# An ODE layer beside an eigenvector recurrence: its matrix scaled first, longer turns, and merge-tree signs without levels

## The chip, the core and the metric

The kernel runs on one core of one Trainium2 chip. The metric is device time in microseconds from launch to end; lower is better. The program is eight layers over one activation tensor, and the change touches one stage of it.

## What is computed

The input `x` has shape (16, 512, 128), the adjacency `adj` (512, 512). Each layer adds its result to `x`. Two layers meet in the stage of this case: layer L1's graph part, eight Euler steps of an ODE, and the eigenvectors `U` that layer L2's graph part needs, which depend on `adj` alone and are computed beside the earlier layers.

```python
def _L1_gnn_ref(x, adj_mx, alpha_train, w, d, fc_in_w, fc_in_b, vt):
    ...
    h = jnp.einsum('bnd,ed->bne', x, fc_in_w) + fc_in_b
    alph = jax.nn.sigmoid(alpha_train)[:, None]
    ...
    def euler_step(h, _):
        ax = jnp.einsum('nm,bmd->bnd', adj_mx, h)
        f = alph * 0.5 * (ax - h) + h @ w_eff - h + x0
        return (h + dt * f, None)
...
    _, U = jnp.linalg.eigh(L_norm)
...
    x = x + _L1_gnn_ref(_layernorm(x, axis=-1), adj, L1_gnn_alpha_train, L1_gnn_w, L1_gnn_d, L1_gnn_fc_in_w, L1_gnn_fc_in_b, 0)
```

## The kernel before, in words

`eigenvectors` (L757) has two stages before its last one. The first finds the eigenvalues of a tridiagonal matrix by counting sign changes. The second, the `nc.Block` at L1140, is the stage of this case. It turns eigenvalues into eigenvectors `Z` (512 per partition, four column blocks `NB` = 4), nearly all on VectorE (DVE):

- **entry** (L1161 to L1187): a root and some scaling, among it L1181, which scales the 128x2048 matrix `V` that only the next stage reads;
- **recurrence** (L1207 to L1225): 512 steps `n`, each of three dependent 128x8 operations (L1213, L1221, L1223), and every 16 steps two operations for the next diagonals `dn` (L1202);
- **selection and scans** (L1233 to L1289): wide operations; then the squared norms go to ScalarE (ACT) at L1295, which takes their root at L1155, and DVE goes on at L1297 with `dve.wait_ge(root_out, 2)`;
- **merge tree** (L1317 to L1441): signs are decided level by level for blocks of 16, 32, ... 256 entries. Each of the five levels issues 48 DVE operations on 128x64, 128x32, ... 128x4 elements, and every one waits for the one ahead of it. At the end L1443 gives `Z` its signs.

Beside it runs class `Ode` (L2783). TensorE (PE) does its matrix work, ACT copies results out of PSUM, and DVE does small pieces of it in between its own steps:

- `Ode.start` (L2835), on DVE, ahead of the recurrence: 64 `bn_stats` (L2840) for the layer norm of `X`; then `wTd` (L2845), the scaled matrix `L1` (L2852, L2855), mean and deviation (the root on ACT, L2992), and `rstd` (L2883).
- **prelude** on PE: four transposes of `L1` (L3027) as soon as all four blocks are there, then 512x512 products for its second, third and sixth power (L3033), small products for powers `R` of the weights (L3039) and rows for the bias (L3062, L3067, L3072). They wait for DVE through `r_in`, `fr_in` and `row_in`.
- **turns**: 17 of them (L3076 to the end of `tensor`), number -1 for the constant term `KC`, then 0 to 15 for the batches. In a turn PE waits for `YT` from ACT, does 12 matmuls of 384 columns (L3083), four transposes (L3089) once DVE's four row blocks (L2889, semaphore `x_full`) are there, then L3095 and L3102 twice. In turn -1 the weights of L3083 are one row of one partition. ACT copies between them (L3007, L3004, L3010, L3015).
- DVE's pieces come from the generator `vector` (L2892). `side.tick()` stands after each recurrence step and after most operations behind it. `yield n` in the generator means that the next piece follows n ticks later, and a turn takes `TURN` = 29 ticks. In a turn DVE does four row blocks, adds `KC` to `X` (L2959) and adds the result of the turn before (L2967). What is left is issued by `side.finish()` at the end.

ACT's program in this stage is `side.scalar(act)`, all of the ODE's copies, between the roots of L1152 and L1155. Its instructions run in that order:

```python
                    nc.scalar.activation(t1[:, :], t1[:, :], ACT.Sqrt).then_inc(root_out, 1)
                    side.scalar(act)
                    act.wait_ge(root_in, 2)
                    nc.scalar.activation(LO[:, :], LO[:, :], ACT.Sqrt).then_inc(root_out, 1)
```

The stage ends for all engines together, when DVE is through and all 16 results are added (`dve.wait_ge(side.added, B)`).

## Time and profile before

| what | value |
|---|---|
| median of 3 runs | 6687.58 us (6683.04 to 6689.84) |
| the profiled execution, its own time | 6687.53 us |
| its span, first to last instruction | 6685.5 us |
| busy: TensorE, VectorE, ScalarE, GpSimd | 79%, 68%, 35%, 1% |
| mean granted TensorE clock | 0.936 |
| the stage of this case | 4078.4 us to 4664.8 us of the span |

All times in what follows are microseconds from the start of the span, unless they are lengths. In a row of a timeline the first number is the start, the second how long the row took (of "x64", all 64 together), and square brackets hold the idle time ahead of it on its engine and what ended it. The profile gives a matmul of f32 as two records, so L3083's 12 matmuls read x24.

### The profile page before, as it was taken

To read this page: it belongs to the slowest core of one execution; us is meant where nothing else is said; L and a number is where in the kernel's file an instruction comes from. 1 tells how busy PE (TensorE), PEld (TensorE's weight loads), DVE (VectorE), ACT (ScalarE), POOL (GpSimd) and SP (SyncE) were. 2 spreads that over 40 slices of the span, in tenths; PEclk is the share of its full clock that TensorE was granted. 3 is DMA by queue.
4 is the path that set the end of the run, shared out by engine and by line. 5 is a ranking of instruction groups with operands and counts; after the bars stand their busy time and mean duration, and the time that the engine had idled before them with its cause. 6 is when DMAs were issued, how large, how long until landed. Compare 5 with 4: busy or idle time off the path is not lost. (4 is left out here: it accounts for less than half of the span.)

```text
span 6685.5 us, 109379 instructions
## 1 busy us (share of the span) xinstructions
PE 5302.8 (79%) x33047; PEld 3780.1 (57%) x33047; DVE 4555.0 (68%) x26992; ACT 2314.4 (35%) x7376; POOL 93.3 (1%) x128
## 2 busy tenths in 40 slices
PE   4666788888877769969899995995573689976999
PEld 4555566666666535446566662663351367745676
DVE  7888888888888863359999998778445333345333
ACT  2222222222222224529598893110020133311333
POOL 0000000000000000000000000000000000000000
PEclk9999999999999999969999997997786889986999
DMA  1000000000000000010000000000010000000000
GB/s 47 2 2 2 2 3 5 3 4 4 3 4 4 4 21 13 7 54 4 5 6 5 6 3 8 1 1 1 1 51 1 13 0 0 0 10 14 0 0 25
DMA packets 27827, 56.64 MB, mean 8 GB/s; under 512 B 6185, under 2 KB 16834, under 8 KB 25538
## 3 DMA queue, kind: packets, MB, share of 16 engines
q1 hardware_dynamic: 27330, 50.79, 2.2%
q8 instruction: 216, 3.54, 0.2%
q14 instruction: 281, 2.30, 0.1%
HBM read 38.20 MB, written 12.58 MB: 8 GB/s over the span
## 5 line engine op out<-in xcount | busy, mean ns | idle before, releaser
L2007 DVE SCALAR_TENSOR_TENSOR f_ACC<-f_yp,f_CG,f_ACC 128x128 f32<-128x128 f32 x1024 | 288.4, 344 | 461.6 <-DVEq L2005 461.6
L1952 PEld LDWEIGHTS f_yp<-f_W,f_hs 128*128 128x128 f32 x4096 | 490.1, 192 | 92.5 <-issue 91.8
L1886 PE MATMUL f_hp<-f_rows,f_W 128*128 128x512 f32 x1024 | 532.3, 602 | 4.8 <-ACT U L1896 2.7
L1983 ACT ACTIVATE f_hs<-f_hp,f_b 128x512 f32<-128x512 f32 x512 | 347.6, 685 | 539.9 <-ACTq L1982 539.9
L710 PE MATMUL h_small<-h_part,ones 128*128 128x2 f32 x1024 | 300.8, 363 | 294.1 <-DVE h_jd L579 198.1
L1054 ACT ACTIVATE e_XD<-e_X,e_scal 128x60 f32<-128x60 f32 x2048 | 527.7, 333 | 17.5 <-DVEq L918 15.7
L655 ACT ACTIVATE h_VW<-h_v,h_s 128x8 f32<-128x8 f32 (+3 forms) x512 | 154.9, 302 | 1082.4 <-DVE h_s L417 1082.4
L1942 PE MATMUL f_hp<-f_XT,f_W 128*128 x1024 | 484.5, 601 | 33.1 <-PEq L2236 33.1
L703 PEld LDWEIGHTS h_ax<-h_XM,h_parts 128*128 128x128 bf16 x11520 | 481.0, 114 | 40.9 <-issue 40.9
L1952 PE MATMUL f_yp<-f_W,f_hs 128*128 128x128 f32 x4096 | 493.5, 275 | 0.0
L710 PEld LDWEIGHTS h_small<-h_part,ones 128*128 128x128 f32 x1024 | 256.8, 312 | 414.7 <-DVE h_jd L579 287.2
L703 PE MATMUL h_ax<-h_XM,h_parts 128*128 128x3 bf16 x11520 | 407.9, 167 | 30.0 <-DVE h_parts L170 30.0
L678 PE MATMUL h_small<-h_part,ones 128*128 128x2 f32 x1024 | 300.5, 363 | 159.4 <-DVE h_jb L337 122.0
L678 PEld LDWEIGHTS h_small<-h_part,ones 128*128 128x128 f32 x1024 | 256.7, 311 | 289.2 <-DVE h_jb L337 232.7
L692 PE MATMUL h_sr<-h_sums,ones 128*128 128x1 f32 (+15 forms) x1024 | 314.9, 397 | 79.6 <-DVE h_parts L170 42.5
L1876 PEld LDWEIGHTS f_yp<-f_W,UT 128*128 128x128 f32 x2048 | 267.4, 195 | 187.6 <-issue 92.6
L1876 PEld LDWEIGHTS f_yp<-f_W,U 128*128 128x128 f32 x2048 | 268.6, 192 | 113.9 <-issue 92.8
L692 PEld LDWEIGHTS h_sr<-h_sums,ones 128*128 128x128 f32 x1024 | 256.9, 311 | 104.3 <-issue 48.6
L1876 PE MATMUL f_yp<-f_W,UT 128*128 128x128 f32 x2048 | 281.5, 282 | 40.5 <-ACT UT L1896 32.2
L2754 PE MATMUL g_PG<-g_HL,g_Wih 128*128 128x256 f32 (+2 forms) x624 | 291.8, 625 | 21.9 <-DMA g_bhh<-in_g_bhh 18.0
L641 ACT ACTIVATE h_s<-h_small 128x1 f32<-128x1 f32 x512 | 87.7, 171 | 580.4 <-PE h_small L678 579.7
L939 DVE SCALAR_TENSOR_TENSOR e_PB<-e_PB,e_scal,e_u 128x60 f32<-128x60 f32 x1024 | 283.1, 276 | 0.0
(715 smaller groups left out, 11303.0 us busy)
## 6 DMA issues: line engine op xcount, KB each, us to landing
f_S<-in_f_W SPq DMA_DIRECT2D x64, 128.0 KB, 2.3
X<-in_x SPq DMA_DIRECT2D x1, 4096.0 KB, 16.4
held<-g0e_HL SPq DMA_DIRECT2D x16, 256.0 KB, 2.0
g_HL<-held SPq DMA_DIRECT2D x16, 256.0 KB, 2.8
f_W<-in_f_W SPq DMA_DIRECT2D x2, 2048.0 KB
spill<-f_xts SPq DMA_DIRECT2D x16, 256.0 KB, 2.0
f_rows<-spill SPq DMA_DIRECT2D x16, 256.0 KB, 2.6
f_W<-in_f_W SPq DMA_DIRECT2D x4, 1024.0 KB
```

Source lines behind the costliest of these rows:

```text
L678: nc.tensor.matmul(tot[j % 2], C.ones[:, :], part[:, 0:2], start=True, stop=True).then_inc(tot_out, 1)
L692: nc.tensor.matmul(sr[:, 0:n], C.ones[:, :], sums[:, 0:n], start=True, stop=True).then_inc(sr_out, 1)
L703: ins = nc.tensor.matmul(ax[:, m, 0:3], A_part[:, b, m * P:(m + 1) * P], XB[:, q, b, 2 * XC + 1:2 * R2 + 2:2], start=(b == ph and n == 0), ...
L710: nc.tensor.matmul(dots, C.ones[:, :], part[:, 2:4], start=True, stop=True).then_inc(dots_out, 1)
L1054: ins = nc.scalar.activation(XD[b][:, k, h, :], X[:, :], ACT.Identity, bias=scal[b][:, k, 2 * h:2 * h + 1])
L1876: ins = nc.tensor.matmul(self.yp[d % 3][:, 0:D], self.hs[unit % 2][:, j, i * P:(i + 1) * P], self.W2[:, unit % E * FC + j, :], start=(j == ...
L1886: nc.tensor.matmul(self.hp[s % 3][:, :], self.W1[:, e, j * P:(j + 1) * P], self.rows[:, g % 2, :], start=True, stop=True).then_inc(self.h_ ...
L1942: nc.tensor.matmul(hp[:, u % 2, c, :], W1[:, col // F, col % F:col % F + P], rows_t, start=True, stop=True).then_inc(h_full, 1)
L1952: ins = nc.tensor.matmul(yp[:, u % 2, k, :], hs[:, u % 2, c, k * P:(k + 1) * P], W2[:, u * UC + c, :], start=(c == 0), stop=(c == UC - 1))
L1983: nc.scalar.activation(hs[:, u % 2, c, :], hp[:, u % 2, c, :], func, bias=b1[:, u * UC + c:u * UC + c + 1]).then_inc(hs_full, 1)
L2007: ins = V_.scalar_tensor_tensor(ACC[:, k, :], yp[:, u % 2, k, :], CG[:, k * E + e:k * E + e + 1], ACC[:, k, :], ALU.mult, ALU.add)
L2754: ins = nc.tensor.matmul(o2, Wih[:, p - 1, gi * D:(gi + 1) * D], x, start=True, stop=(t == 0))
```

## The change

Three parts, in one stage.

**The order at its start.** `side.start` stands ahead of L1181 and no longer holds the 64 `bn_stats`. These and the rest of the layer norm are in a new `side.statistics`, behind the scaling of `V`. Row 1 and row 2 of the weight powers are made there, not in ticks. ACT takes the deviation's root behind the copies of `L1T` and `L2T`.

```diff
@@ -1178,6 +1188,7 @@
                     dve.wait_ge(ch, done.next())
                     V_.tensor_tensor(G[:, :], rad[:, :], t1[:, :], ALU.mult).then_inc(ch, 1)
                     dve.wait_ge(ch, done.next())
+                    side.start(dve)
                     V_.tensor_tensor(V[:, :, :], V[:, :, :], G[:, :].unsqueeze(1).broadcast_to([P, NB, N]), ALU.mult).then_inc(ch, 1)
                     dve.wait_ge(ch, done.next())
                     V_.memset(EB[:, 0:1], 0.0).then_inc(ch, 1)
@@ -1186,8 +1197,32 @@
                     done.next()
                     V_.memset(one[:, :], 1.0).then_inc(ch, 1)
                     dve.wait_ge(ch, done.next())
-                    side.start(dve)
+                    side.statistics(dve)
                     side.begin(dve)
```

**The pacing of the ODE's pieces.** `TURN` goes from 29 to 34, with 12 more in turn -1. The generator waits fewer ticks ahead of the powers (12 and 6 in place of 4, 17, 17 and 17). The one copy of `Fr` moves behind the products of `Gm`. Single ticks behind wide operations become 2, 4 or 6.

```diff
@@ -2784,7 +2816,7 @@


     STEPS = 8
-    TURN = 29
...
@@ -2835,10 +2867,6 @@
     def start(self, dve):

         V_, ch, done, C = self.nc.vector, self.ch, self.done, self.C
-        st, a, b, v, mean, rstd = (t[:, :] for t in (self.st[:, :, 0], self.a, self.b, self.v, self.mean, self.rstd))
-        for t in range(T):
-            V_.bn_stats(self.st[:, t, :], self.X[:, t, :]).then_inc(ch, 1)
-            done.next()
...
             V_.scalar_tensor_tensor(blk, C.ident[:, :], self.a78[:, n:n + 1], blk, ALU.mult, ALU.add).then_inc(self.l1_made, 1)
+        V_.tensor_copy(self.R[:, 0, :], C.ident[:, :]).then_inc(ch, 1)
+        done.next()
+
+    def statistics(self, dve):
+
+        V_, ch, done = self.nc.vector, self.ch, self.done
+        a, b, v, mean, rstd = (t[:, :] for t in (self.a, self.b, self.v, self.mean, self.rstd))
+        dve.wait_ge(self.r_out, 1)
+        V_.tensor_scalar(self.R[:, 1, :], self.PR[:, 0:D], 1.0 / self.STEPS, None, ALU.mult).then_inc(self.r_in, 1)
+        for t in range(T):
+            V_.bn_stats(self.st[:, t, :], self.X[:, t, :]).then_inc(ch, 1)
+            done.next()
+        dve.wait_ge(ch, done.n)
...
         V_.tensor_tensor(v, a, b, ALU.add).then_inc(self.var_in, 1)
-        V_.tensor_copy(self.R[:, 0, :], C.ident[:, :]).then_inc(ch, 1)
-        done.next()
+        self.wider_power(dve, 0)
...
+    def wider_power(self, dve, k):
+
+        lo, hi = ((2, 3), (3, 5), (5, 9))[k]
+        dve.wait_ge(self.r_out, k + 2)
+        self.nc.vector.tensor_copy(self.R[:, lo:hi, :].rearrange("p m d -> p (m d)"), self.PR[:, 0:(hi - lo) * D]).then_inc(self.r_in, 1)
...
@@ -2893,18 +2939,14 @@

         V_, ch, done, C, STEPS = self.nc.vector, self.ch, self.done, self.C, self.STEPS
         R, Gm, Fr, PR, TY = self.R, self.Gm, self.Fr, self.PR, self.TY
-        dve.wait_ge(self.r_out, 1)
-        V_.tensor_scalar(R[:, 1, :], PR[:, 0:D], 1.0 / STEPS, None, ALU.mult).then_inc(self.r_in, 1)
         for n in range(NB):
             ins = self.row_block(0, n)
             if n == NB - 1:
                 ins.then_inc(self.x_full, 1)
             yield 2
-        yield 4
-        for k, (lo, hi) in enumerate(((2, 3), (3, 5), (5, 9))):
-            dve.wait_ge(self.r_out, k + 2)
-            V_.tensor_copy(R[:, lo:hi, :].rearrange("p m d -> p (m d)"), PR[:, 0:(hi - lo) * D]).then_inc(self.r_in, 1)
-            yield 17
+        for k in (1, 2):
+            self.wider_power(dve, k)
+            yield 12 if k == 1 else 6
...
                     ins.then_inc(self.fr_in, 1)
             yield 2
-        dve.wait_ge(self.frow_out, 3)
-        V_.tensor_copy(Fr[:, STEPS, :], PR[0:1, 0:D]).then_inc(ch, 1)
-        done.next()
...
                 if k % 4 == 3:
                     yield 1
+        yield 3
+        dve.wait_ge(self.frow_out, 3)
+        V_.tensor_copy(Fr[:, STEPS, :], PR[0:1, 0:D]).then_inc(ch, 1)
+        done.next()
+        yield 9
...
                 V_.tensor_tensor(xs, xs, self.HS[(turn - 1) % 2], ALU.add).then_inc(self.added, 1)
-            yield self.TURN - used
+            yield self.TURN + (self.LEAD if turn < 0 else 0) - used
...
-    def tick(self):
-
...
+    def tick(self, times=1):
+
+        for _ in range(times):
+            if self.pause > 0:
+                self.pause -= 1
+            if self.pause == 0:
+                self.pause = next(self.work, -1)
...
         nc.scalar.activation(self.al[:, :], self.al[:, :], ACT.Sigmoid).then_inc(self.sg, 1)
-        act.wait_ge(self.var_in, 1)
-        nc.scalar.activation(self.sd[:, :], self.v[:, :], ACT.Sqrt).then_inc(self.sd_out, 1)
         for out, made, full in ((self.L1T, self.l1t_out, self.l1t_in), (self.L2T, self.l2t_out, self.l2t_in),
                                 (self.L3T, self.l3t_out, self.l3t_in), (self.L3, self.l3_out, self.l3_in),
                                 (self.L6T, self.l6t_out, self.l6t_in)):
+            if out is self.L3T:
+                act.wait_ge(self.var_in, 1)
+                nc.scalar.activation(self.sd[:, :], self.v[:, :], ACT.Sqrt).then_inc(self.sd_out, 1)
```

```diff
                         done.next()
-                        side.tick()
+                        side.tick(2)
                     dve.wait_ge(ch, done.n)
                     V_.tensor_tensor(g1[:, :, :], bwd, g1[:, :, :], ALU.subtract).then_inc(ch, 1)
-                    side.tick()
+                    side.tick(6)
                     dve.wait_ge(ch, done.next())
                     V_.scalar_tensor_tensor(g1[:, :, :], g1[:, :, :], -1.0, g1[:, :, :], ALU.mult, ALU.max).then_inc(ch, 1)
...
                         V_.memset(t2[:, 0:1], 0.0).then_inc(ch, 1)
-                        side.tick()
                         dve.wait_ge(ch, done.next())
                         V_.scalar_tensor_tensor(t2[:, 1:N], ES[:, 0:N - 1], -1.0, R[:, N - 2::-1, NB + jb], ALU.mult, ALU.mult).then_inc(ch, 1)
-                        side.tick()
+                        side.tick(2)
                         dve.wait_ge(ch, done.next())
                         V_.tensor_tensor_scan(Z[:, jb, :], t2[:, :], t1[:, :], 0.0, ALU.mult, ALU.add).then_inc(ch, 1)
-                        side.tick()
+                        side.tick(2)
```

**The merge tree.** What depends on `ES` and the tolerances alone is made ahead of the recurrence. All 31 nodes of the five levels stand side by side in tensors of 31 per column block (128x124). Everything but the signs is computed for all of them at once, with waits only where an input needs one. A node's sign is written as `sa * (sb * p + r) + (sb * s + q)`, and only these six operations are done level by level.

```diff
                     V_.tensor_tensor(g1[:, :, :], Z[:, :, :], Z[:, :, :], ALU.mult).then_inc(ch, 1)
-                    dve.wait_ge(ch, done.next())
-                    V_.tensor_reduce(mass[:, :, :], g1[:, :, :].rearrange("p j (s w) -> p j s w", w=LEAF), AX.X, ALU.add).then_inc(ch, 1)
-                    dve.wait_ge(ch, done.next())
+                    done.next()
                     V_.memset(sg[:, :, :], 1.0).then_inc(ch, 1)
-                    dve.wait_ge(ch, done.next())
...
-                        size *= 2
...
+                    side.tick(2)
+                    dve.wait_ge(ch, done.n)
+                    V_.tensor_tensor(host[:, :, :], ma, mb, ALU.is_ge).then_inc(ch, 1)
+                    host_made = done.next()
+                    V_.tensor_tensor(a2[:, :, :], va[:, :, :], vb[:, :, :], ALU.subtract).then_inc(ch, 1)
+                    a2_made = done.next()
+                    V_.tensor_tensor(mx[:, :, :], ma, mb, ALU.mult).then_inc(ch, 1)
+                    mx_made = done.next()
+                    V_.tensor_tensor(mh[:, :, :], ma, mb, ALU.max).then_inc(ch, 1)
+                    mh_made = done.next()
+                    V_.tensor_scalar(st[:, :, :], tt[:, :, :], 0.0, -2.0, ALU.is_ge, ALU.mult).then_inc(ch, 1)
+                    st_made = done.next()
+                    dve.wait_ge(ch, max(host_made, a2_made))
+                    V_.tensor_tensor(a2[:, :, :], a2[:, :, :], host[:, :, :], ALU.mult).then_inc(ch, 1)
+                    a2_made = done.next()
+                    dve.wait_ge(ch, mx_made)
+                    V_.tensor_scalar(mx[:, :, :], mx[:, :, :], tol[:, 0:1], 0.64, ALU.mult, ALU.mult).then_inc(ch, 1)
+                    mx_made = done.next()
+                    dve.wait_ge(ch, mh_made)
+                    V_.tensor_scalar(mh[:, :, :], mh[:, :, :], tol[:, 0:1], None, ALU.mult).then_inc(ch, 1)
...
+                    dve.wait_ge(ch, max(mx_made, k2_made))
+                    V_.scalar_tensor_tensor(sp[:, :, :], k2[:, :, :], -1.0, mx[:, :, :], ALU.mult, ALU.mult).then_inc(ch, 1)
+                    done.next()
+                    V_.scalar_tensor_tensor(sq[:, :, :], k2[:, :, :], 1.0, mx[:, :, :], ALU.subtract, ALU.mult).then_inc(ch, 1)
+                    done.next()
+                    side.tick(4)
+                    for size, lo, hi in levels:
+                        w = hi - lo
+                        dve.wait_ge(ch, done.n)
+                        V_.tensor_tensor(x1[:, :, 0:w], sb_[:, :, lo:hi], sp[:, :, lo:hi], ALU.mult).then_inc(ch, 1)
+                        u_made = done.next()
+                        V_.tensor_tensor(mh[:, :, 0:w], sb_[:, :, lo:hi], ss[:, :, lo:hi], ALU.mult).then_inc(ch, 1)
+                        w_made = done.next()
+                        dve.wait_ge(ch, u_made)
+                        V_.tensor_tensor(x1[:, :, 0:w], x1[:, :, 0:w], sr[:, :, lo:hi], ALU.add).then_inc(ch, 1)
+                        u_made = done.next()
+                        dve.wait_ge(ch, w_made)
+                        V_.tensor_tensor(mh[:, :, 0:w], mh[:, :, 0:w], sq[:, :, lo:hi], ALU.add).then_inc(ch, 1)
+                        w_made = done.next()
+                        dve.wait_ge(ch, u_made)
+                        V_.tensor_tensor(x1[:, :, 0:w], x1[:, :, 0:w], sa[:, :, lo:hi], ALU.mult).then_inc(ch, 1)
+                        u_made = done.next()
+                        dve.wait_ge(ch, max(u_made, w_made))
+                        V_.tensor_tensor(sg[:, :, LEAVES + lo:LEAVES + hi], x1[:, :, 0:w], mh[:, :, 0:w], ALU.add).then_inc(ch, 1)
+                        done.next()
+                        side.tick(2)
+                    dve.wait_ge(ch, done.n)
                     for jb in range(NB):
-                        V_.tensor_scalar(Z[:, jb, :], Z[:, jb, :], sg[:, jb, 0:1], None, ALU.mult).then_inc(ch, 1)
-                        dve.wait_ge(ch, done.next())
+                        V_.tensor_scalar(Z[:, jb, :], Z[:, jb, :], sg[:, jb, 2 * LEAVES - 2:2 * LEAVES - 1], None, ALU.mult).then_inc(ch, 1)
+                        done.next()
```

How this moves the instructions, at three places. **DVE at the stage's entry**, where `e_Z` is the matrix `L1` and `t_V` is `V`. Before:

```order
L1181 TENSOR_TENSOR t_V<-t_V,t_G 128x2048 [waits e_chain]
L1183 MEMSET e_EE 128x1 [waits e_chain]
L1185 COPY e_EE<-e_EE 128x511
L1187 MEMSET e_one 128x8
L2840 BN_STATS g_st<-X 128x6 [waits e_chain]
L2840 BN_STATS g_st<-X 128x6 x63
L2843 TENSOR_SCALAR g_d<-g_d 128x1 [waits g1_loaded]
L2845 TENSOR_SCALAR g_wTd<-g_wT,g_d 128x128 [waits g1_ch]
L2847 TENSOR_SCALAR g_a<-g_al 128x4 [waits g1_sg]
L2849 TENSOR_SCALAR g_a<-g_a 128x4 [waits g1_ch]
L2852 TENSOR_SCALAR e_Z<-e_Z,g_a 128x512 [waits g1_ch]
L2855 SCALAR_TENSOR_TENSOR e_Z<-ident,g_a,e_Z 128x128 [waits g1_ch]
```

and now, from the fourth and last block of the matrix on (L2880, L2883):

```order
L2880 TENSOR_SCALAR e_Z<-e_Z,g_a 128x512
L2883 SCALAR_TENSOR_TENSOR e_Z<-ident,g_a,e_Z 128x128 [waits g1_ch]
L2884 COPY e_g<-ident 128x128
L1192 TENSOR_TENSOR t_V<-t_V,t_G 128x2048
L1194 MEMSET e_EE 128x1 [waits e_chain]
L1196 COPY e_EE<-e_EE 128x511
L1198 MEMSET e_one 128x8
L2892 TENSOR_SCALAR e_g<-g_PR 128x128 [waits g1_r_out,e_chain]
L2894 BN_STATS g_st<-X 128x6 x64
L2898 TENSOR_TENSOR g_ln_a<-g_st 128x64 [waits g1_ch]
```

The scaled matrix now stands ahead of the scaling of `V` and of the statistics.

**ACT**, whose `g_ln_sd` is the deviation of the layer norm and `e_LO` the root of the squared norms. The change, at the start of the stage:

```order
L3035 ACTIVATE g_al<-g_al 128x4 [waits g1_loaded]
L3044 COPY g_L1T<-g_Q 128x512 [waits g1_l1t_out] x4
L3044 COPY U<-g_Q 128x512 [waits g1_l2t_out] x4
L3041 ACT_TABLE_LOAD
L3041 ACTIVATE g_ln_sd<-g_ln_v 128x64 [waits g1_var_in]
L3044 COPY g_L3T<-g_Q 128x512 [waits g1_l3t_out] x4
```

and at its end:

```order
L3050 COPY g_YT<-g_TY 128x512 [waits g1_ty_out]
L3053 COPY UT<-g_Q 128x512 [waits g1_q_out]
L3056 COPY UT<-g_Q 128x512 [waits g1_v_out]
L3061 COPY UT<-g_Q 128x512 [waits g1_added,g1_h_out]
L1165 ACTIVATE e_LO<-e_LO 128x4 [waits e_root_in]
```

The root of the deviation moved behind eight copies. The root of `e_LO` is where it was, last, behind every copy of the ODE.

**DVE, the last level of the signs and the end** (`s_sg` are signs). Now:

```order
L1456 TENSOR_TENSOR s_w<-s_sg,s_w 128x4 [waits e_chain]
L1458 TENSOR_TENSOR s_w<-s_sg,s_w 128x4
L1461 TENSOR_TENSOR s_w<-s_w 128x4 [waits e_chain]
L1464 TENSOR_TENSOR s_w<-s_w 128x4 [waits e_chain]
L1467 TENSOR_TENSOR s_w<-s_w,s_sg 128x4 [waits e_chain]
L1470 TENSOR_TENSOR s_sg<-s_w 128x4 [waits e_chain]
L1475 TENSOR_SCALAR e_Z<-e_Z,s_sg 128x512 [waits e_chain]
L1475 TENSOR_SCALAR e_Z<-e_Z,s_sg 128x512 x3
L3011 TENSOR_TENSOR X<-X,UT 128x512 [waits g1_hs_in,g1_ch]
```

A level issues 6 operations here, where it issued 48, and the last addition to `X` is now behind the signs.

## Rows read from the trace of the kernel before

**Rows 1.** The page's first line.

```profile
span 6685.5 us, 109379 instructions
```

**Rows 2.** Stretches: length, busy time (instructions) of PE, PEld, DVE, ACT, POOL, PE clock, DMA.

```profile
4078.40:4665.00 586.60, 450.99 (x1978) 285.34 (x1978) 452.89 (x2182) 72.82 (x126) 0.00 (x0) 0.88 0.01 3
4603.77:4662.53 58.76, 0.00 (x0) 0.00 (x0) 50.16 (x249) 0.00 (x0) 0.00 (x0) 0.50 0.00 0
```

**Rows 3.** Waits of DVE in the stage: us in total, times, longest.

```profile
DVE g_XG L2889 <- PE g_TY L3102: 58.2, 14, 12.7
```

**Rows 4.** Timeline of DVE in the entry: scaling of `V`, then the ODE's first operation.

```profile
4087.04 2.29 DVE L1181 TENSOR_TENSOR t_V<-t_V,t_G 128x2048 f32<-128x2048 f32 x1
...
4102.24 0.13 DVE L2843 TENSOR_SCALAR g_d<-g_d 128x1 f32<-128x1 f32 x1
```

**Rows 5.** Groups of the entry on DVE: busy, mean ns of one, idle before.

```profile
L2840 DVE BATCH_NORM_STATS2 g_st<-X 128x6 f32<-128x128 f32 x64 | 12.5, 273 | 0.0
```

**Rows 6.** Timeline of PE in the prelude, from its second bias row to turn -1.

```profile
4157.14 1.86 PE L3062 MATMUL g_PR<-e_g,g_fbC 128*1 128x512 f32 x2 [12.06 <-DVE e_g L2924]
4158.93 15.01 PE L3033 MATMUL g_Q<-g_L3T,UT 128*128 128x512 f32 x32
...
4177.52 3.60 PE L3072 MATMUL g_TY<-g_L6T,ones 128*1 128x512 f32 x8
4186.11 15.72 PE L3083 MATMUL g_Q<-e_g,U 1*128 1x384 f32 x24 [4.99 <-DVEq L2944]
```

**Rows 7.** Timeline of ACT in the prelude.

```profile
4084.64 1.28 ACT L2992 ACT_TABLE_LOAD   x1
...
4125.12 0.58 ACT L2998 COPY U<-g_Q 128x512 f32<-128x512 f32 x1 [2.85 <-PE g_Q L3033]
```

**Rows 8.** Timeline of DVE in the prelude: weights `Gm`, then the first bias row.

```profile
4152.60 0.64 DVE L2913 TENSOR_SCALAR g_Gm<-g_TY 128x128 f32<-128x128 f32 x3
...
4156.28 0.80 DVE L2924 TENSOR_SCALAR e_g<-g_PR 1x128 f32<-1x128 f32 x4
```

**Rows 9.** Timeline of DVE in a turn: row blocks, an addition, two plain steps.

```profile
4243.47 0.29 DVE L2889 TENSOR_SCALAR g_XG<-X,g_mean,g_rstd 128x128 f32<-128x128 f32 x1
...
4244.20 0.30 DVE L2889 TENSOR_SCALAR g_XG<-X,g_mean,g_rstd 128x128 f32<-128x128 f32 x1
4244.41 0.16 DVE L1213 SCALAR_TENSOR_TENSOR e_t<-e_QR,e_EE 128x8 f32<-128x8 f32 x1
...
4245.48 0.16 DVE L1213 SCALAR_TENSOR_TENSOR e_t<-e_QR,e_EE 128x8 f32<-128x8 f32 x1
...
4246.12 0.17 DVE L1213 SCALAR_TENSOR_TENSOR e_t<-e_QR,e_EE 128x8 f32<-128x8 f32 x1
```

**Rows 10.** Timeline of PE: the first matmuls of turns 0 and 1.

```profile
4218.82 8.01 PE L3083 MATMUL g_Q<-g_Gm,g_YT 128*128 128x384 f32 x24 [0.68 <-ACT g_YT L3004]
...
4242.45 8.01 PE L3083 MATMUL g_Q<-g_Gm,g_YT 128*128 128x384 f32 x24 [0.68 <-ACT g_YT L3004]
```

**Rows 11.** Stretches of turn -1 and turn 0 on PE: length, busy, PE clock, DMA.

```profile
4186.10:4201.80 15.70, 15.69 (x25) 0.50 0.00 1
...
4218.80:4226.80 8.00, 7.98 (x26) 1.00 0.00 0
```

**Rows 12.** Timeline: ACT's last copy of the ODE, DVE at the root.

```profile
4590.44 0.58 ACT L3015 COPY UT<-g_Q 128x512 f32<-128x512 f32 x1 [3.93 <-PE g_Q L3095]
...
4599.76 0.17 DVE L1295 COPY e_LO<-e_q 128x4 f32<-128x4 f32 x1
...
4600.20 0.18 DVE L1297 RECIPROCAL e_q<-e_LO 128x4 f32<-128x4 f32 x1 [0.27 <-ACT e_LO L1155]
```

**Rows 13.** Timeline of DVE in the merge tree, first level, and its end.

```profile
4612.26 0.23 DVE L1361 TENSOR_TENSOR s_w<-s_w 128x64 f32<-128x64 f32 x1
4612.52 0.23 DVE L1363 TENSOR_TENSOR s_w<-s_w 128x64 f32<-128x64 f32 x1
...
4662.53 2.05 DVE L1443 TENSOR_SCALAR e_Z<-e_Z,s_sg 128x512 f32<-128x512 f32 x4
```

More of the change, by code:

```diff
@@ new lines, in _ @@
+                    V_.tensor_reduce(mass[:, :, 0:LEAVES], g1[:, :, :].rearrange("p j (s w) -> p j s w", w=LEAF), AX.X, ALU.add).then_inc(ch, 1)
+                    mass_made = done.next()
+                    V_.tensor_tensor(tt[:, :, :], vb[:, :, :], st[:, :, :], ALU.mult).then_inc(ch, 1)
+                    made = done.next()
+                    V_.tensor_tensor(vb[:, :, :], vb[:, :, :], vb[:, :, :], ALU.mult).then_inc(ch, 1)
+                    vb_made = done.next()
+                    dve.wait_ge(ch, made)
@@ new lines, in _ @@
+                    side.tick(2)
+                    dve.wait_ge(ch, done.n)
[6 more added lines that the diff above has]
+                    V_.tensor_tensor(mh[:, :, :], ma, mb, ALU.max).then_inc(ch, 1)
@@ new lines, in _ @@
+                    x1_made = done.next()
+                    dve.wait_ge(ch, a2_made)
+                    V_.scalar_tensor_tensor(a2[:, :, :], a2[:, :, :], 2.0, bb4, ALU.mult, ALU.mult).then_inc(ch, 1)
+                    a2_made = done.next()
+                    dve.wait_ge(ch, st_made)
+                    V_.tensor_scalar(st[:, :, :], st[:, :, :], 1.0, None, ALU.add).then_inc(ch, 1)
+                    st_made = done.next()
+                    side.tick(4)
+                    dve.wait_ge(ch, max(a2_made, mh_made))
@@ new lines, in _ @@
+                    side.tick(4)
+                    for size, lo, hi in levels:
+                        w = hi - lo
[15 more added lines that the diff above has]
+                        V_.tensor_tensor(sg[:, :, LEAVES + lo:LEAVES + hi], x1[:, :, 0:w], mh[:, :, 0:w], ALU.add).then_inc(ch, 1)
+                        done.next()
+                        side.tick(2)
@@ L2938, in vector @@
                     yield 1
+        yield 3
+        dve.wait_ge(self.frow_out, 3)
+        V_.tensor_copy(Fr[:, STEPS, :], PR[0:1, 0:D]).then_inc(ch, 1)
+        done.next()
+        yield 9
         for j in (1, 2):
```

219 lines of the change are left out of this document (93 added, 126 removed).

## The prediction, made before the change was run

> **What bounds the kernel now.** I first asked which part of the span the change can touch. It is one stage of 586.6 us out of 6685.5, with DVE busy 452.9 and PE 451.0 of it [rows 1, 2]. Nothing of any other stage moves, and a barrier closes this one, so the question is only when the stage ends. The waits of DVE come next. It sat idle for 58.2 us in 14 waits of its row blocks for PE [rows 3]: in each turn of the ODE DVE is done first and waits. PE's turns follow each other every 23.63 us [rows 10], and PE waits 0.68 at each start, for ACT. So in the recurrence PE is the bound and DVE waits. Then it turns round. ACT's last copy of the ODE ends at 4591.0, and DVE comes to the root only at 4599.8 [rows 12]. From there on PE is idle and DVE alone runs until 4664.6: 64.4 us, of which the merge tree takes 58.8 for 249 instructions [rows 2, 12, 13]. The stage's end is therefore: PE's turns, then a gap of 9 us, then DVE's tail.
>
> **The chain after the change.** DVE arrives at the root earlier, since the longer turns let it do five more steps per turn in place of waiting. A turn of DVE is now 34 steps of 0.64 us, 21.8; four row blocks add 0.09 each (0.73 against 0.64), two additions 0.43 each (1.07 against 0.64) [rows 9], and the diagonals about 0.3. Together 23.3, just under PE's 23.63. By the same count the old 29 steps are 20.1, and 13 waits of 3.5 and one of 12.7 are the 58.2 of the row. Without them DVE would arrive at 4599.8 - 58.2 = 4541.6, give or take a few microseconds for pieces that move. But the root on ACT still stands behind all of the ODE's copies, so DVE cannot pass it before the last turn is over. What was hidden becomes a wait of some 24 us. The new chain is: scaled matrix, PE's prelude, 17 turns, ACT's last copy and root, DVE's tail. So I need three sizes: how much earlier turn -1 starts, what it costs, and how long the tail is. Adding up DVE's savings (58 in the turns, 42 in the tail) would count 24 us that the root gives back.
>
> **1. The scaled matrix comes first: 15.2 us.** Its first operation goes from 4102.24 to 4087.04, where the scaling of `V` began [rows 4]. This takes 64 `bn_stats` (12.5 [rows 5]), the scaling (2.3) and two short ones from in front of PE. They aren't gone, they lie beside PE's first products. The deviation's root is now late: it waits for ACT's eight copies, the last of which ended at 4125.7 before, so 4110.5 now, and for a table load of 1.28 [rows 7]. With the root, the five operations behind it and 13 small ones for the tree's constants (an estimate of 3.4) the recurrence starts at about 4115.2. DVE pays for that out of its 24.
>
> **2. The rest of the prelude: 3.1 and 4.2 us.** PE's second bias row waits for DVE's first four `Fr` operations. They now stand behind 30 steps, `Gm` behind 27. 27 steps are 17.3, and the pieces between them about 1.8, so `Gm` starts at 4134.3; from there to the end of `Fr` it was 4152.60 to 4157.08, 4.5 [rows 8]. So PE goes on at 4138.8 in place of 4157.14 [rows 6], 18.3 earlier, 3.1 more than the start gave: most of the wait of 12.06 stays. From there PE's own work to its last bias row took 24.0 (4157.14 to 4181.12), then it waited 4.99 [rows 6]. The products of `Gm` that held it up are done earlier now; a copy of one row and the hand-over stay, some 0.8. Turn -1 starts at 4138.8 + 24.0 + 0.8 = 4163.6 in place of 4186.1: **22.5 us earlier**. The first 2 us of the product in this stretch ran at half clock (15.01 for 32 records); a wait of another length can move this by 2 either way.
>
> **3. Turn -1: 3 us, between 0 and 7.7.** Its matmuls with weights of one row took 15.72 for 24 records at half the clock, 1.2 GHz; the same count at 2.4 GHz takes 8.01 [rows 6, 11]. PE had idled 4.99 ahead of them. Now it idles 0.8, behind work at the full clock, so it should enter at 2.4 GHz. But for 15.7 us of unbroken work the clock did not rise [rows 11], so such matmuls don't seem to hold it either, and it will fall on the way. I take 3, nearer to the row of the same matmuls than to the full gain. The Trainium skill, TensorE: Matmul & The Clock Gate (What's actually happening), says that the clock is set by how busy PE has been of late, and that a busy PE gets 2.4 GHz. By it this turn would run at the full clock and the sum would be 6606; this trace disagrees, with 15.69 of 15.70 us busy at 0.50.
>
> The sixteen turns behind it don't change, since DVE's 23.3 stays under 23.63, and its row blocks are wanted only 7.8 into PE's turn. The end of the ODE goes from 4591.0 to 4591.0 - 22.5 - 3 = 4565.5, and with the root (0.3 to DVE's next operation) DVE goes on at 4565.8 in place of 4600.2.
>
> **4. The tail: 64.4 becomes 22.8, 41.6 us.** A chained operation of 128x64 takes 0.23 and the next starts 0.26 after it [rows 13]. An operation that waits for nothing starts before the one ahead of it ends: 64 `bn_stats` of 273 ns are busy for 12.5 us in all, one each 195 ns [rows 5], and four row blocks add little to their steps. In the new order I count 91 operations. Up to the scaled `Z` nothing changes but one addition: 3.6. The squares 2.2, a memset and ten copies at 0.1 each 1.2, an addition 0.6, the reduction 2.2: 6.2. Then 28 operations on 124 elements, an estimate of 0.29 each from the row of 64 elements and one ns for each element more, but each 0.08 under the next, so 5.9, and four sums of masses 0.5. Five levels of signs with six short operations, 0.9 each, 4.5. Signs into `Z` 1.6, the last addition 0.65. Sum 22.9, rounded in the parts to 22.8. If nothing overlapped, some 70 of them would cost 0.12 more each: 8.3.
>
> The Trainium skill speaks against this part: VectorE: DVE Perf Modes (Rules for kernel authors, and The DRAIN you can't avoid) says that a drain between Vector operations comes whether or not they wait for a semaphore, and that their count matters, not their waits. By it the tail would be those 8.3 longer and the kernel 6619.5. The trace disagrees at `bn_stats`, and the page's own section on two instructions with no wait between them allows the earlier start.
>
> **Sum.** The stage ends at 4565.8 + 22.8 = 4588.6 in place of 4664.6: 76.0 us less. Against the profiled execution's own 6687.5 that is 6611.5; its time is that of the median (6687.58), so nothing is to be shifted. The recounted parts lie on either side of it by half a microsecond; I say 6611.
>
> **The rivals.**
> - *Turn -1 at the full clock* (7%): 4.7 us better than I take, 6606. For it: PE enters warm. Against it: [rows 11].
> - *Waits cost nothing, so dropping them gives nothing* (5%): 6619.5. Against it: [rows 5].
> - *The prelude stays as long as it was* (6%): a new wait of PE, or a product at half clock behind its idle time. The 7.3 us of part 2 and the 3 of part 3 are lost, 6622. For it: PE still waits on DVE's ticks there, about 9 us, and the root of the deviation is now on DVE's way.
> - *The root doesn't hold DVE* (2%): DVE's own pace sets the end, 4541.6 + 0.4 + 22.8 = 4565 and 6588. It would need ACT to be through with the ODE at 4541.6; the order of ACT's instructions speaks against it.
> - *Slower: DVE becomes late in every turn and the clock falls in each* (2%). 34 steps leave 0.3 us of a turn. If the row blocks came late, PE would idle in each turn; an idle time of 4.99 was followed by half clock, one of 0.68 was not [rows 6, 10]. With the clock down at each L3083 the sixteen turns cost 16 x 7.7 = 123 us, the sum turns from -76 to +47, 6734. It decides from an idle time of about 5 us per turn, so with steps of about 0.79 us and not 0.64 [rows 9].
> - That the change doesn't do what it says I hold for excluded: the new order has the matrix first and six operations in a level.
>
> **How the numbers follow.** The forecast has 77%. Its own bounds are 2 for the clock in the prelude, 1.5 for the 30 steps, 3 and 4.7 for turn -1, 1 for the tail, and the three runs before lie 7 us apart. This gives 6603 to 6620, which also holds the cases of 6606 and 6619.5; that leaves out about 1 in 7. A measurement here tells no more than about 0.2% (13 us) from no change, and only the slower case and unnamed mishaps are not better by that: faster 0.97, within 0.2% 0.01, slower 0.02.
>
> **What would show it.** In the new profile: the first transposes of PE at 4091; the second bias row near 4139; the first matmul of turn -1 near 4163.6, and the clock's stretch over it between 0.5 and 1.0; turns of 23.63 still; the waits of DVE for its row blocks under 6 us in all in place of 58.2; a new wait of DVE at the root of about 24 us for ACT; the stage from there in 22.8. Wrong would be: a wait of PE for `x_full`, no wait at the root, or operations of the tail that start only after the one ahead has ended.

## The result, and the profile after

The median is 6611.9 us of 4 runs (6609.02 to 6614.83), against 6688.7 of 4 runs of the kernel before: a ratio of 0.9886, 95% interval 0.9869 to 0.9904. The forecast was 6611 in a range of 6603 to 6620. The profiled execution took 6609.97, its span is 6607.7.

The page's first line of the changed kernel, which answers to [rows 1]:

```profile
span 6607.7 us, 109220 instructions
```

Its stage, from DVE's first operation (4079.92) to DVE's last end, and then the part from the root on, as stretches with the columns of [rows 2]:

```profile
4079.80:4590.20 510.40, 451.69 (x1978) 285.62 (x1978) 420.04 (x2021) 72.94 (x126) 0.00 (x0) 0.94 0.01 3
4567.60:4590.10 22.50, 0.00 (x0) 0.00 (x0) 21.79 (x91) 0.00 (x0) 0.00 (x0) 0.60 0.00 0
```

PE does the same 1978 matmul records and is busy 451.7 us with them, before 451.0. DVE has 161 instructions fewer in the stage. **Places in the stage are from here on counted from DVE's first operation in it** (4078.51 before, 4079.92 after), because each execution enters the stage at another moment. So counted, the stage was 586.1 and is 510.2: 75.9 less, where the working had 76.0. The span lost 77.8: the stage was entered 1.4 later, and what stands behind it took 2017.6 in place of 2020.9, with the same instructions. More on that below.

The waits of DVE in the stage (us in total, times, longest), which answer to [rows 3]:

```profile
DVE e_q L1331 <- ACT e_LO L1165: 26.7, 1, 26.7
DVE g_XG L2935 <- PE g_TY L3148: 3.9, 10, 1.9
DVE g_rstd L2915 <- ACT g_ln_sd L3041: 3.5, 1, 3.5
```

The 58.2 us of waits for PE are 3.9, and the root, where DVE waited 0.27, now holds it for 26.7. The timeline of the entry, the prelude, turn -1 and the first two turns, to be laid beside [rows 4, 6, 10]:

```profile
4088.44 0.15 DVE L2871 TENSOR_SCALAR g_d<-g_d 128x1 f32<-128x1 f32 x1
...
4092.52 3.67 PE L3073 MATMUL g_Q<-ident,e_Z 128*128 128x128 f32 x16 [2.75 <-DVE e_Z L2883]
...
4131.27 3.32 PE L3102 MATMUL g_TY<-e_g,g_fc 128*128 128x512 f32 x4 [2.72 <-DVE e_g L2930]
...
4139.51 1.86 PE L3108 MATMUL g_PR<-e_g,g_fbC 128*1 128x512 f32 x2 [3.66 <-DVE e_g L2966]
4141.31 16.03 PE L3079 MATMUL g_Q<-g_L3T,UT 128*128 128x512 f32 x32
...
4165.34 11.85 PE L3129 MATMUL g_Q<-e_g,U 1*128 1x384 f32 x24 [0.83 <-DVEq L2988]
...
4195.24 8.01 PE L3129 MATMUL g_Q<-g_Gm,g_YT 128*128 128x384 f32 x24 [0.68 <-ACT g_YT L3050]
...
4218.88 8.01 PE L3129 MATMUL g_Q<-g_Gm,g_YT 128*128 128x384 f32 x24 [0.68 <-ACT g_YT L3050]
```

The first matmuls of turn -1 took 11.85 in place of 15.72, and turn 0 takes 23.64 as before. And the end of the stage, which answers to [rows 12, 13]:

```profile
4566.88 0.58 ACT L3061 COPY UT<-g_Q 128x512 f32<-128x512 f32 x1 [3.93 <-PE g_Q L3141]
...
4567.60 0.18 DVE L1331 RECIPROCAL e_q<-e_LO 128x4 f32<-128x4 f32 x1 [26.71 <-ACT e_LO L1165]
...
4582.26 0.28 DVE L1439 TENSOR_TENSOR s_w<-s_w 128x124 f32<-128x124 f32 x1
4582.46 0.28 DVE L1442 SCALAR_TENSOR_TENSOR s_w<-s_w 128x124 f32<-128x124 f32 x1
...
4589.40 0.68 DVE L3011 TENSOR_TENSOR X<-X,UT 128x512 f32<-128x512 f32 x1
```

Two operations of 0.28 start 0.20 apart: the second begins before the first has ended. From the root on DVE does 91 operations, where the kernel before did 263 in its 64.4 us.

### The profile page after: what moved, and what is told of

It is laid out like the page before. It is cut to its first block and busy times, and to the rows that moved or that the text cites. A ratio compares the mean times of both kernels' runs of the same rounds, so it can differ in the third digit from the quotient of the medians.

```text
span 6607.7 us, 109220 instructions
## 1 busy us (share of the span) xinstructions
PE 5302.0 (80%) x33047; PEld 3776.1 (57%) x33047; DVE 4521.4 (68%) x26831; ACT 2314.0 (35%) x7376; POOL 93.3 (1%) x128
## 5 line engine op out<-in xcount | busy, mean ns | idle before, releaser
L1054 ACT ACTIVATE e_XD<-e_X,e_scal 128x60 f32<-128x60 f32 x2048 | 527.7, 333 | 17.5 <-DVEq L918 15.7
L2786 PE MATMUL g_PG<-g_HL,g_Wih 128*128 128x256 f32 (+2 forms) x624 | 294.1, 628 | 21.4 <-DMA g_bhh<-in_g_bhh 17.5
```

Source lines behind the costliest of these rows:

```text
L1054: ins = nc.scalar.activation(XD[b][:, k, h, :], X[:, :], ACT.Identity, bias=scal[b][:, k, 2 * h:2 * h + 1])
L2786: ins = nc.tensor.matmul(o2, Wih[:, p - 1, gi * D:(gi + 1) * D], x, start=True, stop=(t == 0))
```

## The experiments

The table gives for each kernel, in us from the start of the stage: the start of turn -1, the end of ACT's last copy of the ODE, DVE's first operation behind the root, and the end of the stage; then the median of the runs. A median with one run is marked 1x. Each ratio, with its 95% interval, is to executions of the kernel before that ran beside that kernel (their medians lie between 6685.8 and 6691.8), so it can differ a little from the quotient of two medians of the table.

| kernel | turn -1 | ODE's end | root | stage | median | ratio |
|---|---|---|---|---|---|---|
| before | 107.6 | 512.5 | 521.7 | 586.1 | 6688.7 | |
| changed | 85.4 | 487.5 | 487.7 | 510.2 | 6611.9 | 0.9886 (0.9869 to 0.9904) |
| tree_only | 110.6 | 515.8 | 524.9 | 546.3 | 6656.7 | 0.9953 (0.9939 to 0.9966) |
| no_tree | 83.1 | 485.2 | 485.4 | 551.1 | 6651.4 | 0.9944 (0.9931 to 0.9958) |
| stats_first | 96.0 | 498.2 | 498.4 | 520.8 | 6630.0 | 0.9912 (0.9898 to 0.9925) |
| turn29_single | 85.3 | 487.5 | 502.3 | 523.2 | 6629.1 | 0.9903 (0.9888 to 0.9918) |
| tree_chained | 85.1 | 487.2 | 487.4 | 521.5 | 6629.4 | 0.9907 (0.9892 to 0.9922) |
| root_early | 85.4 | 487.5 | 462.9 | 488.7 | 6596.1 | 0.9857 (0.9842 to 0.9873) |
| root_early_turn37 | 85.4 | 487.5 | 462.9 | 488.7 | 6594.0 | 0.9848 (0.9833 to 0.9863) |
| root_early_prelude | 81.8 | 483.9 | 460.0 | 485.0 | 6589.3 | 0.9849 (0.9835 to 0.9862) |
| bias_rows_later | 74.1 | 477.9 | 453.4 | 479.1 | 6580.4 | 0.9845 (0.9832 to 0.9859) |
| full_rows | 85.4 | 481.2 | 481.4 | 503.8 | 6613.0 (1x) | |
| uneven_turns | 85.4 | 529.0 | 504.5 | 530.2 | 6635.2 (1x) | |
| tree_only_again | 110.5 | 515.7 | 524.7 | 546.1 | 6650.3 (1x) | |

**1. The tree alone.** The kernel before, with the part of the change on the merge tree only, `TURN` as it was. Of the pacing's diff it has this alone, since the new tree calls `tick` with a number:

```diff
-    def tick(self):
+    def tick(self, times=1):
```

> The kernel before with the new merge tree alone (its constants ahead of the recurrence; the old order at the entry, turns of 29). My theory (ODE, then root, then DVE's tail, the savings in series): DVE still comes to the root at 4600 and the tail shrinks by 41.6, so about 6646. Rival, that an operation costs the same with and without a wait ahead of it: the tail is 8.3 longer, about 6655. In the trace: the tail from the root 22.5 to 23 us; the waits of DVE for its row blocks still 58 or so, less the 1.3 of the constants that they now hide.

The stage is 39.8 shorter. The tail is 21.4 in place of 64.4, 43.0 less (the last addition to `X` is ahead of it here). But the ODE ends 3.3 later than before: the 13 small operations for the tree's constants, 1.3 us, stand ahead of everything DVE owes PE in the prelude, and PE's second bias row starts 2.5 later. They are not hidden by the waits, as I had expected; DVE's waits for its row blocks come later and are still 58.3. Outside the stage this execution took 8.9 us more (8.4 of them behind it), which is why the median is nearer to what the rival gave. The stage decides: the rival wanted a tail 8.3 longer than 22.5, and it is 21.4.

**2. All but the tree.** The changed kernel, with the old tree back, and the constants that it makes itself gone from ahead of the recurrence:

```diff
-                    for size, lo, hi in levels:
-                        V_.tensor_copy(be[:, lo:hi], ES[:, :].rearrange("p (s w) -> p s w", w=2 * size)[:, :, size - 1]).then_inc(ch, 1)
-                        be_made = done.next()
...
+                    while size < N:
+                        m = N // size // 2
...
```

> The changed kernel with the old merge tree (new order at the entry, turns of 34 kept). My theory: the ODE ends as early as in the changed kernel and the root still waits for it, so only the old tail of 64.4 comes back: 6688.7 - 34 = about 6654.5; with the tree alone the two savings add up to the whole. Rival, that 58 us of removed waits of DVE are worth something by themselves: under 6640. In the trace: a wait at the root of 26.7 us as in the changed kernel.

The stage is 35.0 shorter than before, DVE waits 26.7 at the root. Alone, the two halves give 39.8 and 35.0, together 74.8 of the 75.9. The ODE's end is 27.3 earlier than before, and the gap from there to the root shrinks from 9.2 to 0.1. These 9 are all that the 58 us of waits gave: the earlier end of the ODE comes from the entry, the prelude and turn -1.

**3. The order at the entry.**

```diff
+                    side.bn(dve)
+                    side.start(dve)
                     side.statistics(dve)
```

(`bn` holds the 64 `bn_stats`; `side.start` is taken from ahead of the scaling of `V`, and on ACT the deviation's root stands first again.)

> The changed kernel with the old order at the entry: scaling of V and the 64 bn_stats ahead of the scaled matrix, the deviation's root ahead of ACT's copies. My theory: PE starts 15.2 us later and all that hangs on it, so 6612 + 15.2 = about 6627, and the wait at the root shrinks only by what DVE itself loses less. Rival, that the order at the entry is worth nothing because DVE's own work sets the end: 6612. A third, that PE's wait for the bias rows takes some of it back, since DVE's pieces are now nearer to what PE needs: 6612 + 9 or so.

PE's transposes start 15.3 later, as counted. Turn -1 starts only 10.6 later, and the stage is 10.7 longer. The third case came out: with PE later, DVE's pieces come in time. PE's wait for the third power (2.72) is gone, and the matmuls behind it run in 1.88 and not 3.32. So in the final kernel the order at the entry is worth 10.7 of the stage. The 15.2 were right for the start and too much for what it brings in this prelude. The median says more, 18.1: the profiled execution entered the stage 1.7 later and took 6.4 more behind it than the one of the changed kernel (on that part see the last section).

**4. Turns of 29.**

```diff
-    TURN, LEAD = 34, 12
+    TURN, LEAD = 29, 17
...
-                        side.tick(2)
+                        side.tick()
```

> The changed kernel with turns of 29 steps and single ticks behind the wide operations, as before; turn -1 keeps its 46 ticks. My theory: the ODE ends at the same place of the stage (487.5 behind its start), DVE waits 3.5 per turn again and comes to the root at about 496, so the stage is 8 to 9 longer and the time about 6620: of 58 us of waits only these 9 were ever worth anything while the root stands last. Rival, that the longer turns carry the change: the waits of about 55 come back in the time, 6660 or more.

The ODE ends at the same 487.5, DVE waits 44.5 us in 13 turns, and comes to the root at 502.3. The stage is 13.0 longer. So the mechanism holds (44.5 us of waits cost 13.0), and my size for it was 4 to 5 too small. I had moved DVE's arrival before (521.3) by the 25 that turn 0 starts earlier. But DVE also has fewer steps behind it when the turns begin: its 100th reciprocal starts at 122.7 before, 17.6 ahead of turn 0, and here at 117.0, 1.7 behind turn 0. That is 19.3 less of a lead; 13.7 of it come back in the turns (waits of 44.5 in place of 58.2), and the other 5.6 make 496.4 into the 502.0 at which DVE came to the root.

**5. A wait ahead of each operation of the new tree.**

```diff
+                    dve.wait_ge(ch, done.n)
                     V_.tensor_tensor(mx[:, :, :], ma, mb, ALU.mult).then_inc(ch, 1)
```

> The changed kernel with a wait ahead of every operation of the new merge tree, as the old one had; the operations are the same. My theory: what starts 0.08 ahead of the other's end now starts 0.03 behind it, so the tail from the root grows from 22.5 by about 8.3 to 30.8, and the time by as much, to about 6620. Rival, that only the number of operations counts: the tail stays at 22.5 and the time at 6612.

The tail from the root is 34.1 in place of 22.5: 11.7 more. DVE in this tail, wide operations of the same kind as above:

```profile
4572.83 0.29 DVE L1375 TENSOR_TENSOR s_w<-s_w 128x124 f32<-128x124 f32 x1
4573.22 0.29 DVE L1379 TENSOR_TENSOR s_w<-s_w 128x124 f32<-128x124 f32 x1
4573.55 0.29 DVE L1382 TENSOR_TENSOR s_w<-s_w 128x124 f32<-128x124 f32 x1
```

They start 0.32 to 0.33 or 0.39 apart, not 0.20. 0.33 is about what I had counted (the end of the one, and 0.03); 0.39 is where the added wait stands beside one that was already there. The page counts 51 instructions more (109271 against 109220), all of them waits, and 51 at 0.07 are 3.6 of the 11.7; the other 8.1 are close to the 8.3 of the expectation. The number of operations on DVE is the same (91), so the rival is refuted: waits between operations of 128x4 to 128x124 cost. The stage is 11.3 longer than in the changed kernel; the median is 17.5 above, so some 6 of it lie outside the stage.

**6. The root earlier.** On ACT, in `Ode.scalar`; the two lines behind `side.scalar(act)` become `root`.

```diff
             row(1)
+            if g == B - 2:
+                root()
             act.wait_ge(self.h_out, g + 2)
```

> The changed kernel with the root of the squared norms on ACT moved from behind all copies of the ODE to the middle of turn 14 (behind its second copy of YT). My theory: DVE's wait of 26.7 at the root falls to about 2, its tail of 22.5 lies beside PE's last turn, and the stage ends with the last addition, 0.7 after ACT's last copy: 22 us less, about 6590. Rival, that DVE's additions and PE's last turn get in each other's way, or ACT waits for DVE and holds PE up: between 6592 and 6612.

The stage is 21.5 shorter than in the changed kernel, 97.4 shorter than before. The place of the root, and the end of the stage:

```profile
4544.94 0.17 DVE L1330 COPY e_LO<-e_q 128x4 f32<-128x4 f32 x1
4546.40 0.58 ACT L3051 COPY g_YT<-g_TY 128x512 f32<-128x512 f32 x1 [2.85 <-PE g_TY L3151]
4546.88 0.21 ACT L1165 ACTIVATE e_LO<-e_LO 128x4 f32<-128x4 f32 x1
4547.12 0.18 DVE L1332 RECIPROCAL e_q<-e_LO 128x4 f32<-128x4 f32 x1 [2.01 <-ACT e_LO L1165]
...
4571.11 0.58 ACT L3064 COPY UT<-g_Q 128x512 f32<-128x512 f32 x1 [3.93 <-PE g_Q L3144]
4572.15 0.69 DVE L3012 TENSOR_TENSOR X<-X,UT 128x512 f32<-128x512 f32 x1 [3.15 <-ACT UT L3064]
```

DVE's tail lies beside PE's last turn, PE's chain is untouched (turn -1 and the ODE's end at the same places), and DVE waits 3.15 for the last result. This shows that the 26.7 were a wait for an instruction that only stood late in ACT's order, and that the stage is now bounded by the ODE's end.

**7. Turns of 37, with the early root.**

```diff
-    TURN, LEAD = 34, 12
+    TURN, LEAD = 37, 9
```

> The early root with turns of 37 steps (turn -1 still 46 ticks). DVE's turn is then 25.1 against PE's 23.63. My theory: PE waits for the row blocks 1.5 us per turn through some 13 turns, the ODE ends 20 later, at 507 of the stage, and the time is about 6615. Rival, the slower case of my prediction: with PE idle in each turn the clock falls at each turn's first matmuls, and it is 50 to 100 us more. If 37 steps cost nothing, DVE's turn is not what I counted.

A miss: nothing changes, the stage is 488.7 again. DVE's turn is longer than PE's, as counted, but PE does not wait. The last of DVE's row blocks and the last transposes of them on PE, first in the changed kernel, then here:

```profile
4505.87 0.33 DVE L2935 TENSOR_SCALAR g_XG<-X,g_mean,g_rstd 128x128 f32<-128x128 f32 x1
...
4534.02 0.60 PE L3135 MATMUL g_TY<-ident,g_XG 128*128 128x128 f32 x4
```

```profile
4526.80 0.32 DVE L2936 TENSOR_SCALAR g_XG<-X,g_mean,g_rstd 128x128 f32<-128x128 f32 x1
4537.30 0.60 PE L3138 MATMUL g_TY<-ident,g_XG 128*128 128x128 f32 x4
```

The blocks are ready 27.8 ahead of their use in the changed kernel (29.4 to 29.6 in nearly all turns, before as well), and 10.2 ahead here, after falling by about 1.6 a turn from 27.4. They are written into the second of two buffers, a whole turn early. A turn of DVE may be longer than one of PE as long as the sum of the differences stays under 29.

**8. Turns of 50, then of 22, with the early root**, so that this lead is used up.

```diff
-            yield self.TURN + (self.LEAD if turn < 0 else 0) - used
+            yield (46 if turn < 0 else 50 if turn < 7 else 22) - used
```

> The early root with turns of 50 steps up to turn 6 and of 22 from then on: a test of the slower case of my prediction, that a late DVE idles PE in each turn and the clock falls there. DVE's turn of 50 steps is 33.3, so it loses 9.7 per turn. With the lead of 28 to 29 us that the trace shows for the row blocks, PE is held up only from the fourth such turn on, by some 9.7 per turn through three or four turns: 30 to 40 us, a stage of 520 to 530. If the clock falls behind each such idle time, the matmuls behind it show 0.5 and the stage is up to 7 us per held turn longer.

PE waited 34.4 in five turns. Its timeline at the first full one:

```profile
4311.78 8.01 PE L3132 MATMUL g_Q<-g_Gm,g_YT 128*128 128x384 f32 x24 [0.68 <-ACT g_YT L3051]
4330.01 1.12 PE L3138 MATMUL g_TY<-ident,g_XG 128*128 128x128 f32 x4 [10.23 <-DVE g_XG L2936]
4330.92 5.45 PE L3144 MATMUL g_Q<-UT,g_L1T 128*128 128x128 f32 x32
```

Behind an idle time of 10.23 (and of 8.11, 7.82 and 7.56 in the next turns) the transposes take 1.12 in place of 0.60 and the matmuls behind them 5.45 in place of 3.8: the granted clock of this stretch is 0.64, part of it at 1.2 and part at 2.4 GHz. The ODE's end is 41.5 later than with even turns, 34.4 of it waiting. The 7.1 left are some 1.8 for each of the four long waits. So the clock does fall there, and costs 1.8 and not the 7.7 of my slower case. A wait of this length ahead of L3083 did not occur and was not tried.

**9. Turn -1 with 128 rows of weights.**

```diff
-                    left = YT[...] if g >= 0 else self.yrow[...]
-                    right = Gm if g >= 0 else Fr
+                    left = YT[...] if g >= 0 else L1T[...]
+                    right = Gm
```

> The changed kernel with turn -1's first 12 matmuls on weights of 128 rows (L1T and Gm) in place of one row: the constant term KC comes out other than it should. Size and number of the matmuls stay. If weights of one row are what lets the clock fall, these matmuls take 8.0 in place of 11.85, and with the full clock behind them turn 0 starts 5 earlier. If the wait of 0.8 ahead or the phase of the clock does it, they take 11.85 again.

The two kernels as stretches over these matmuls, the changed one and this one:

```profile
4165.30:4177.10 11.80, 11.76 (x24) 5.97 (x24) 10.10 (x58) 0.00 (x0) 0.00 (x0) 0.67 0.01 2
```

```profile
4164.70:4172.50 7.80, 7.77 (x24) 4.62 (x25) 6.74 (x40) 0.00 (x0) 0.00 (x0) 1.00 0.01 3
```

8.01 in place of 11.85, at the full clock, behind the same wait of 0.83. Turn 0 starts 6.3 earlier (109.0 in place of 115.3). PE is as busy in the one stretch as in the other; what differs is that weights and moving data have 128 rows and not one, and their values. That it is the one row, at the same count, width and wait, under which the clock falls is shown by this, as far as the values do not matter; and it was down behind them too (2.5 of the 6.3). Which padding of the real constant term would give this time was not tried.

**10 and 11. Further on the ODE's start, with the early root.** First the tree's constants go where DVE waits for the deviation's root, and the third power follows 8 ticks behind the second:

```diff
         self.wider_power(dve, 0)
+        between()
         dve.wait_ge(self.sd_out, 1)
...
-            yield 12 if k == 1 else 6
+            yield 8 if k == 1 else 6
```

> The early root, and two small moves on DVE: the constants of the merge tree are made while DVE waits 3.5 for the deviation's root (they cost the ODE's start up to 2.3 in the comparison with the old tree), and the last power follows 8 ticks behind the one before it, not 12 (PE waited 2.72 for it). My theory: the ODE is what ends the stage now, so it gains 2 to 4 us, until DVE's own end at about 485 of the stage limits it: about 6592. Rival, that PE's later wait for the bias rows takes it all back: 6596.

3.6 less, at 485.0. Then PE's second bias row goes behind the third product, with turns of 36 (on DVE the second half of the `Fr` copies goes behind the products of `Gm`, and the pause ahead of the last rows is 4 ticks and not 9):

```diff
         for half in range(2):
             if half:
+                pe.wait_ge(self.l3_in, NB)
+                product(L3, L3T, self.l6t_out)
                 pe.wait_ge(self.fr_in, half)
...
             if j == 2:
+                pe.wait_ge(self.fr_in, 2)
+                nc.tensor.matmul(PR[0:1, 0:D], self.fbC[:, :], R[:, 0, :], start=True, stop=True).then_inc(self.frow_out, 1)
                 pe.wait_ge(self.l6t_in, NB)
```

> The early root with the small moves of the run before it, turns of 36, and in the prelude PE's second bias row behind the third 512x512 product and the third between the two sums of columns, with DVE's copies moved to match. PE no longer waits 4.6 for DVE ahead of that product. My theory: turn -1 starts 7.3 earlier, the ODE ends at 476.6 of the stage, and now DVE's own work sets the end: it comes to the root at 457 to 458 and its tail of 21.8 ends at 479 to 480. So 5 to 6 us less than 485, about 6584. Rival, that the clock takes it back in turn -1 or DVE's copies come late: 6589.

The stage ends at 479.1. Turn -1 starts 7.7 earlier, but takes 14.13 for its first matmuls where the run before had 11.72, and the ODE's end gains 6.0. The product itself, behind no idle time, now takes 14.00 and not 16.16. I had expected DVE's work to be the bound; it is still the ODE, with DVE waiting 3.1 for the last result. This version beats both kernels: 6580.4 (5 runs, the slowest 6588.5, where the fastest of the changed kernel was 6609.0), a ratio of 0.9845 to before. Its stage is 107 us shorter than before and 31 shorter than in the changed kernel.

**12. The tree alone, once more.**

> The same kernel as the tree alone, for a second profile. The part of its span behind the stage was 2029.3 us, 8.6 more than in the kernel before, with the same instructions. If that belongs to the moment at which the kernel comes out of the stage, it is 2029 again; if it differs from execution to execution, it is some other value between 2017 and 2030.

The stage repeats within 0.2 us (546.1 against 546.3). What stands behind it took 2026.1, against 2029.3 in the first execution.

## Why the prediction was right

It went by the steps of its sum. Places are again counted from the start of the stage.

- **The chain** (ODE, root, DVE's tail in series) is what the trace and the runs 2, 4 and 6 show. The wait at the root was put at 24 and is 26.7; DVE arrived 2.1 earlier than the 4541.6 of the text. That this came so near is partly luck: the text took all 58.2 as gone, where 3.9 were left, and did not count another wait of DVE for PE, 13.2 at L2929 before (for the bias row of L3067) and 2.2 after.
- **The matrix first:** the first operation at 8.52 in place of 23.73, 15.2 as said. PE's transposes are at 12.6, where 4091 meant 12.5. What this part is worth in the end, 10.7, is less (run 3); the text had not claimed more than the start, and summed the prelude in its own term.
- **The prelude:** second bias row at 59.6 (text 60.3), turn -1 at 85.4 (text 85.1): 22.2 earlier, where 22.5 was forecast. Two errors nearly cancel here: PE went on 0.7 sooner than the text said, and the product behind its wait took 16.03 in place of 15.01, for which the text had allowed 2 either way. I had missed PE's wait of 2.72 for the third power and the half clock behind it (3.32 for matmuls of 1.88): they are hidden, because PE would have waited for the bias row anyway. The root, the five operations behind it and the tree's constants, 3.4 in the text, took 3.2 (4113.16 to 4116.32), 1.3 of them the constants.
- **Turn -1:** it began at 2.4 GHz and fell on the way, as the text has it: the granted clock was 1.00 in its first 4.0 us (4165.3 to 4169.3) and 0.50 in the other 7.8. Its first matmuls gained 3.9, the ones behind them, still partly at half clock, gave 1.1 back. Net 2.8 (32.7 to 29.9), where 3 was forecast. The reason given, that weights of one row do not hold the clock, is shown by run 9. What the Trainium skill says in TensorE: Matmul & The Clock Gate (What's actually happening), that a busy engine gets 2.4 GHz, does not hold for them: they ran at 0.67 with PE busy 11.76 of 11.80 us.
- **The tail:** 22.5, forecast 22.8. By run 5, 8.1 of the 41.9 gained come from the overlap, which the text put at 8.3 (the 3.6 of doubled waits are of run 5 alone). The rest comes with the smaller number of operations, 91 in place of 263. The rule in the Trainium skill's VectorE: DVE Perf Modes (Rules for kernel authors), that in a chain of operations the count matters and not the semaphores, is at odds with run 5: the same operations took 11.7 us more with the waits put back.
- **The sum** 76.0, measured 75.9. Its terms were off by more than that: prelude and turn -1 together gained 0.5 less, the tail 0.3 more. That the median (6611.9) lies so near to 6611 is partly luck: the parts of the program that are the same spread by more than the error of the sum.

One argument was wrong, in the slower rival: "34 steps leave 0.3 us of a turn". This took a turn as a race that starts anew each time. Rows of the same kind as [rows 9, 10], of a block's end and of its transposes, would have shown a lead of 29.6. With turns of 37 nothing was lost, and once the lead was used up, the clock took 1.8 for each long wait and not 7.7. The 7.7 came from turn -1, whose 15.7 us at half clock run 9 puts down to weights of one row; with the full weights of the other turns the clock was back within the transposes and the 32 records behind them (run 8). The rival deserved less than its 2%. The same mistake of thought was in my expectation of run 7, and in that of run 4 I left out where DVE stands against PE's turns.

## What to carry to other kernels

When waits are taken from an engine that is not the bound, ask first what instruction on another engine it will run into: here 58 us of waits in the turns turned into 26.7 at the root, and moving that one instruction on ACT gave 21.5 more. An engine that works ahead through two buffers has slack that adds up over turns; read it as the distance between the end of the piece and its use, not as the difference of two periods. For a change in one stage, compare the stage from its own start: that repeated within 0.2 us, while the part ahead of it and the part behind it each varied by 10 us or more over the kernels.

## What the runs showed of the hardware that I had not expected

- The part behind the stage has the same instructions in all kernels, and took 2017.6 to 2029.3 us in the 14 profiled executions (2020.9 before, 2017.6 after, 2029.3 and 2026.1 for two executions of one kernel). Some of it is in the first 142 us: there the three executions before, after and tree_only needed 141.6, 137.3 and 145.1 to the same instruction, with granted clocks of 0.59, 0.77 and 0.67 in the first 20 us. Over the whole part PE does the same 8027 matmul records, and they keep it busy for 1588 us in the two shortest profiles (changed, no_tree) and for 1598 to 1599 in the two longest (tree_only, full_rows): nearly all of the 10 us between them is in matmuls that take longer, as they do at half clock. What decides how much of this part runs at half clock is open. It may go with the kernel, since the five runs of tree_only lie within 1.5 us of each other, but tree_only_again, the same kernel, took 6.4 less.
- Matmuls with weights of one row took 11.7 to 15.7 us for 24 records, depending on what PE did before; with 128 rows 8.01.
- Two waits ahead of one DVE operation cost 0.07 us more than one (0.39 and 0.32 from start to start, run 5).
